# Later batches of x stored turned but unsplit, split when they come back, and setup's stores in another order

## What is computed

```python
proj = x @ W_in.T + b_in                      # W_in (3072, 256): q, k, v
q, k = _rope(q, sin, cos), _rope(k, sin, cos)
att = jnp.einsum('bhqd,bhkd->bhqk', q, k) * scale
att = jax.nn.softmax(jnp.where(mask, att, -inf), axis=-1)   # causal
y = jnp.einsum('bhqk,bhkd->bhqd', att, v)
...
return y @ W_out.T + b_out
x = _layernorm(x + attention(x))
x = _layernorm(x + experts(x))
```

## Time and profile before

| | us |
|---|---|
| median of 3 runs | 1839.72 |
| range of the runs | 1834.96 to 1841.53 |
| the profiled execution | 1837.63 |
| its span | 1834.3 |
| PE busy in the span | 1686.4 (92%) |
| DVE busy | 1383.9 (75%) |
| ACT busy | 722.0 (39%) |
| POOL busy | 1233.9 (67%) |

### The profile page before, as it was taken

The page is one execution under the profiler, slowest core; times in us unless marked ns, Lnnn a source line. Parts: engine busy times, 40 slices in busy tenths (PEclk is TensorE's granted clock), DMA queues, the critical chain, the costliest instruction groups (busy, mean ns, idle before and its releaser), DMA issues. The chain is left out here.

```text
span 1834.3 us, 34020 instructions
## 1 busy us (share of the span) xinstructions
PE 1686.4 (92%) x9515; PEld 1264.3 (69%) x9516; DVE 1383.9 (75%) x3235; ACT 722.0 (39%) x1519; POOL 1233.9 (67%) x1064
## 2 busy tenths in 40 slices
PE   4689999999999999999999999998659999999990
PEld 3556667666766677666766676664339999999980
DVE  3578888888888888988888898875776566656654
ACT  2234444444445544444444444543332222222222
POOL 3256788677877777788767787764017777777764
PEclk8799999999999999999999999999759999999995
DMA  9976556655665676456666565542974444444448
GB/s 307 336 207 162 154 168 199 182 164 157 184 163 156 209 205 179 140 160 187 199 188 187 166 188 142 161 127 98 355 241 72 71 73 74 71 73 74 71 65 278
DMA packets 185058, 302.36 MB, mean 165 GB/s; under 512 B 23120, under 2 KB 82384, under 8 KB 184800
## 3 DMA queue, kind: packets, MB, share of 16 engines
q1 hardware_dynamic: 161360, 269.20, 49.7%
q0 software_dynamic: 21504, 30.29, 10.4%
q10 hardware_dynamic: 2064, 1.31, 0.3%
HBM read 188.81 MB, written 111.67 MB: 164 GB/s over the span
## 5 line engine op out<-in xcount | busy, mean ns | idle before, releaser
L780 ACT ACTIVATE prob<-b_ps 128x512 f32<-128x512 f32 (+3 forms) x768 | 354.4, 488 | 360.3 <-PE b_ps L589 260.3
L516 POOL TENSOR_TENSOR acc<-acc,prob 128x1024 f32<-128x1024 f32 (+1 forms) x192 | 352.8, 1837 | 6.4 <-POOL acc L516 3.6
L588 PE MATMUL b_ps<-q,k 128*128 128x512 f32 (+3 forms) x768 | 296.1, 390 | 5.3 <-ACT prob L780 3.5
L489 POOL TENSOR_TENSOR roped<-rot 128x512 f32<-128x512 f32 x128 | 174.5, 1364 | 165.0 <-DVE rot L919 164.2
L581 PE MATMUL a_ps<-k,q 128*128 128x512 f32 (+3 forms) x768 | 265.8, 383 | 20.5 <-DMA k<-scratch_hilo 10.1
L670 PE MATMUL y_ps<-prob,v_sb 128*64 128x512 f32 (+3 forms) x1536 | 272.9, 490 | 0.1
L899 DVE CUSTOM_DVE_ANT_0 masked<-a_ps,causal 128x128 bf16<-128x128 f32 (+3 forms) x512 | 237.3, 479 | 45.9 <-PE a_ps L581 37.7
L589 PE MATMUL b_ps<-q,k 65*128 65x512 f32 (+3 forms) x768 | 264.4, 348 | 0.0
L1449 POOL DMA_INDIRECT scratch_sum<-y,dst_i x112 | 187.6, 1675 | 94.8 <-ACT y L1521 90.9
L948 DVE RECIPROCAL inv<-inv 128x128 f32<-128x128 f32 x256 | 232.2, 929 | 7.7 <-ACT inv L821 5.3
L494 POOL TENSOR_TENSOR lo<-roped,hi 128x512 fp32r<-128x512 f32 x128 | 176.8, 1382 | 80.6 <-ACT hi L793 80.6
(11 more groups left out here) (255 smaller groups left out, 2382.9 us busy)
## 6 DMA issues: line engine op xcount, KB each, us to landing
q<-scratch_hilo SPq DMA_DIRECT2D x192, 256.0 KB, 4.6
k<-scratch_hilo SPq DMA_DIRECT2D x192, 256.0 KB, 5.2
scratch_hilo<-hi SPq DMA_DIRECT2D x64, 512.0 KB, 3.8
scratch_hilo<-lo SPq DMA_DIRECT2D x64, 512.0 KB, 4.5
w_sb<-scratch_wsplit SPq DMA_DIRECT2D x32, 512.0 KB, 3.6
w<-in_L_ffn_W_dram SPq DMA_DIRECT2D x32, 512.0 KB, 9.9
wv_sb<-scratch_wsplit SPq DMA_DIRECT2D x16, 512.0 KB, 5.9
xT<-scratch_xsplit SPq DMA_DIRECT2D x6, 1024.0 KB, 6.2
```

Of the source, the lines that this page charges most:

```text
L516: nc.gpsimd.tensor_tensor(sums, old, probs(q), ALU.add).then_inc(m["sum_p"], 1)
L588: nc.tensor.matmul(out, k1[s][:, h, js], q1[s][:, h, qs], start=True, stop=False, skip_group_check=True)
L780: nc.scalar.activation(probs(q)[:, h, :], b_ps[:, h, 0:w], ACT.Exp).then_inc(exp_done[h], 1)
```

## The change

Batches 1, 2 and 3 of x are turned in setup and copied out of PSUM whole, in fp32, with no subtraction. They lie in `v_sb` (batch 1) and `prob` (2 and 3) and are stored in `xturned`, 1 MB each in one transfer. `load_x` brings a half of the tokens of such a batch (0.5 MB in place of 1 MB) into the low part of `xT`. There a new event, `s`, splits it: for each of the two k, ACT copies it to the high part, and DVE subtracts. `s0` and `s1` (the halves of the tokens) stand in the lists of ACT and DVE for the pair two turns ahead, and do something only where that pair is the first of a batch other than the first. F0 and F1 of such a pair wait for the split.

In setup, the six weight units that lie in buffers of pair 0 (`WAITED`: q and k of pairs 2 to 7) are stored first, with a semaphore of their own. The stacked loads of pair 0 wait only for these. The other six units (`OTHERS`) are stored in two groups of three, around the first stack. The halves of the second half of the tokens go out after them, and x last, in the order 2, 3, 1. PE no longer waits for the low parts of late units, and ACT no longer waits for the weight stores ahead of batch 3.

```diff
-ACT_ORDER = parse("""E0.0 E0.1 E1.0 E1.1 E2.0 w1 E2.1 E3.0 d1- h0++ N1- E3.1 E4.0 E4.1 y0 h1++ E5.0 d0 h2++ E5.1 E6.0 N0 E6.1 y1 E7.0
+ACT_ORDER = parse("""E0.0 E0.1 s0++ E1.0 E1.1 E2.0 w1 E2.1 E3.0 d1- s1++ h0++ N1- E3.1 E4.0 E4.1 y0 h1++ E5.0 d0 h2++ E5.1 E6.0 N0 E6.1 y1 E7.0
...
-DVE_ORDER = parse("""M11.1 M0.0+ C0 M0.1+ M1.0+ M1.1+ M2.0+ k0 M2.1+ M3.0+ k1 k2 r0++ M3.1+ R4- r1++ R5- M4.1+ k3 M4.0+ R6- R7-
+DVE_ORDER = parse("""M11.1 M0.0+ C0 M0.1+ s0++ M1.0+ M1.1+ M2.0+ k0 M2.1+ M3.0+ k1 k2 s1++ r0++ M3.1+ R4- r1++ R5- M4.1+ k3 M4.0+ R6- R7-
...
+        x_whole = [None] + [t.rearrange("p (k c) -> p k c", k=DK)
+                            for t in (v_flat[:, 0:DK * T], prob[:, 0:DK * T], prob[:, DK * T:2 * DK * T])]
...
+            def put_weights(units, stored):
+                for i in units:
...
+            put_weights(WAITED, wsp_first)
...
             def put_x(b):
                 sp.wait_ge(m["setup_hi"], NW + 4 * (b + 1))
-                sp.wait_ge(m["setup_lo"], NW + 4 * (b + 1))
-                dst = xsplit[b].rearrange("p (a k c) -> p a k c", a=2, k=DK)
-                for a in range(2):
-                    for k in range(DK):
-                        sp.dma_start(dst[:, a, k], x_place[b][a][k].bitcast(F32)).then_inc(xsp[b], 16)
+                sp.dma_start(xturned[b].rearrange("p (k c) -> p k c", k=DK), x_whole[b]).then_inc(xsp[b], 16)
...
             def load_x(batch, c):
-                sp.dma_start(xT[:, :, :, 512 * c:512 * c + 512].bitcast(F32),
-                             row(xsplit, batch).rearrange("p (a k c) -> p a k c", a=2, k=DK)
-                             [:, :, :, 512 * c:512 * c + 512]).then_inc(x_ld[c], 16)
+                sp.dma_start(xT[:, 1, :, 512 * c:512 * c + 512].bitcast(F32),
+                             row(xturned, batch).rearrange("p (k c) -> p k c", k=DK)
+                             [:, :, 512 * c:512 * c + 512]).then_inc(x_ld[c], 16)
...
-            for c in range(2):
-                put_halves(0, 0, c)
-            sp.wait_ge(m["wsp"], 16 * NW)
-            for c in range(2):
-                for second in range(2):
-                    stack(0, 0, c, second)
-                put_x(1 + c)
-            put_x(3)
+            put_halves(0, 0, 0)
+            put_weights(OTHERS[:3], m["wsp"])
+            sp.wait_ge(wsp_first, 16 * len(WAITED))
+            for second in range(2):
+                stack(0, 0, 0, second)
+            put_weights(OTHERS[3:], m["wsp"])
+            put_halves(0, 0, 1)
+            for second in range(2):
+                stack(0, 0, 1, second)
+            for b in (2, 3, 1):
+                put_x(b)
+            sp.wait_ge(m["wsp"], 16 * len(OTHERS))
...
-                    pe.wait_ge(m["setup_lo"], old + 1)
+                    if u < EARLY:
+                        pe.wait_ge(m["setup_lo"], old + 1)
...
-                        if q < 2 and not first:
-                            pe.wait_ge(x_ld[q], 16 * (n // PAIRS + 1))
+                        if q < 2 and n >= PAIRS:
+                            pe.wait_ge(m["setup_lo"], EARLY + splits_before(n, q) + 2)
...
+                    elif kind == "s":
+                        if n % PAIRS or n == 0:
+                            continue
+                        act.wait_ge(x_ld[q], 16 * (n // PAIRS + 1))
+                        for k in range(DK):
+                            nc.scalar.activation(xT[:, 0, k, 512 * q:512 * q + 512],
+                                                 xT[:, 1, k, 512 * q:512 * q + 512].bitcast(F32),
+                                                 ACT.Copy).then_inc(m["setup_hi"], 1)
...
+                    elif kind == "s":
+                        if n % PAIRS or n == 0:
+                            continue
+                        for k in range(DK):
+                            dve.wait_ge(m["setup_hi"], NW + NX + splits_before(n, q) + k + 1)
+                            low = xT[:, 1, k, 512 * q:512 * q + 512]
+                            nc.vector.tensor_tensor(low, low.bitcast(F32), xT[:, 0, k, 512 * q:512 * q + 512].bitcast(F32),
+                                                    ALU.subtract).then_inc(m["setup_lo"], 1)
...
-                        if n == 0 and q == 3:
-                            low_halves(EARLY, NW + NX)
```

More of the change, by code:

```diff
@@ L133, in attention_phase @@
     x, W_in, b_in, W_out, cosT, sinT = A["x"], A["W_in"], A["b_in"], A["W_out"], A["cos"], A["sin"]
-    xsplit, wsplit = dram["xsplit"], dram["wsplit"]
+    xturned, wsplit = dram["xturned"], dram["wsplit"]
     hilo = dram["hilo"]
@@ L189, in attention_phase @@
         m = {k: sem(k) for k in names}
-        xsp = [sem(f"xsp{b}") for b in range(B)]
+        wsp_first = sem("wsp_first")
+        xsp = [None] + [sem(f"xsp{b}") for b in range(1, B)]
         x_in = [sem(f"x_in{b}") for b in range(B)]
@@ L234, in attention_phase @@
                            next(later).rearrange("p (a k c) -> p a k c", a=2, k=DK))
[L235 to L241, removed]
+        v_flat = v_sb[:, 1].rearrange("p t s c -> p (t s c)")
+        x_whole = [None] + [t.rearrange("p (k c) -> p k c", k=DK)
+                            for t in (v_flat[:, 0:DK * T], prob[:, 0:DK * T], prob[:, DK * T:2 * DK * T])]
         def setup_places(u):
@@ L247, in setup_places, with splits_before @@
             b, k, c = X_UNITS[u - NW]
-            return [x_place[b][a][k][:, 512 * c:512 * c + 512] for a in range(2)]
+            cs = slice(512 * c, 512 * c + 512)
+            return [xT[:, a, k, cs] for a in range(2)] if b == 0 else [x_whole[b][:, k, cs]]
+        WAITED = [u for u in range(NW) if W_UNITS[u][0] == "qk" and 2 <= W_UNITS[u][1]]
+        OTHERS = [u for u in range(NW) if u not in WAITED]
+        def splits_before(n, c):
+            return 4 * (n // PAIRS - 1) + 2 * c
         late_banks = [b_ps[:, i, :] for i in range(2)] + [a_ps[:, i, :] for i in range(2)]
@@ L301, in _ @@
             sp.dma_start(wo_raw, W_out.rearrange("(r p) c -> p r c", p=P)).then_inc(m["wo_in"], 16)
[L303 to L307, removed]
+            def put_weights(units, stored):
+                for i in units:
+                    what, p = W_UNITS[i]
+                    sp.wait_ge(m["setup_hi"], i + 1)
+                    sp.wait_ge(m["setup_lo"], i + 1)
+                    sp.dma_start(wsplit[p if what == "qk" else PAIRS + p].rearrange("p (a k c) -> p a k c", a=2, k=DK),
+                                 w_place[i].bitcast(F32)).then_inc(stored, 16)
+            put_weights(WAITED, wsp_first)
             sp.wait_ge(m["setup_hi"], EARLY)
@@ L384, in turn @@
                     elif kind == "S":
-                        if n == 1 and c == 0:
-                            for b in range(1, B):
-                                sp.wait_ge(xsp[b], 64)
                         stack(n, s, c // 2, c % 2)
@@ L544, in late_transposes @@
                     transposes(NW + NX + i, [wo_raw[:, r, (4 * c + j) * P:(4 * c + j + 1) * P] for j in range(4)])
-                pe.wait_ge(m["setup_lo"], NW + NX)
                 pe.wait_ge(m["wo_ev"], len(WO_UNITS))
@@ L734, in high_halves @@
                     act.wait_ge(m["setup_tr"], u + 1)
-                    if u >= NW and X_UNITS[u - NW] == (3, 0, 0):
-                        act.wait_ge(m["wsp"], 16 * NW)
                     src = setup_bank(u)
@@ L762, in turn @@
                             for b in range(1, B):
-                                act.wait_ge(xsp[b], 64)
+                                act.wait_ge(xsp[b], 16)
                         act.wait_ge(b_fill[h], UNITS * n + q + 1)
@@ L1759, in scratch @@
 def scratch(nc):
-    shapes = {"xsplit": [B, P, 2 * DK * T], "wsplit": [PAIRS + PAIRS // 2, P, 2 * DK * 256], "hilo": [2, 2, P, 2, T], "xn": [NTOK, E_ + D]}
+    shapes = {"xturned": [B, P, DK * T], "wsplit": [PAIRS + PAIRS // 2, P, 2 * DK * 256], "hilo": [2, 2, P, 2, T], "xn": [NTOK, E_ + D]}
     shapes.update({f"sum{i}": [NTOK + P, D] for i in range(SUMS)})
```

## The result

| | before | after |
|---|---|---|
| median of four runs each, us | 1838.12 (1834.96 to 1841.53) | 1861.85 (1858.54 to 1864.55) |
| ratio after/before | | 1.0121, 95% interval 1.0104 to 1.0138 |
| profiled execution, its span, us | 1837.6, 1834.3 | 1864.55, 1860.8 |

The change costs 23.7 us. The forecast was 1850, its range ended at 1857. The direction was right, the size wasn't, and what follows is mainly about the twelve microseconds that the forecast lacked.

The account below looks back on a forecast made before the run. Queues bound the first 120 us, and PE, without slack, the turns. 1837.6 - 5.6 (start) - 0.3 (x loads) + 15.6 (splits) + 1.6 (clock) = 1848.9, by the median 1851.0; forecast 1850 us, 8-in-10 range 1838 to 1857.

Parts of the forecast that it names:

- the two holds: Boundary turns: PE held 2.1 us by the first split group, 3.1 by the second; +15.6 us over three boundaries.
- The turns of about 42 us: Predicted trace sign: turns of 36.7 us except three of about 42, those before batches 1, 2 and 3.
- rival (a): Boundary turns: the splits hide in DVE and ACT idle time, costing +2.0 to +3; 1834 us; chance 0.15.
- the term of the clock: Boundary turns: PE's granted clock falls after the 3.1 us hold; up to 1.6 a boundary, a third taken, +1.6 us.
- Rival (c): Boundary turns: the clock falls at both holds and stays low through a fill each; 1857 us; chance 0.08.
- the start: Setup and first turns: reordered stores, dropped subtractions and shorter queue waits gain 5.6 us, between -2 and -11.
- the x loads: Boundary turns: halving the load of x gives at most 0.2 us a boundary; -0.3 taken for the three.
- The wait of 4.24: Start, at 75.81 us: PE's wait for a stacked load; removal gives 0.3, late second stack gives back 0.7.
- The give-back: Start: the second stack lands at about 73 against a need at 71.8, returning up to 1.2 of 4.0 us.
- The two later waits on stacked loads: Start: PE's waits of 0.96 and 2.02 us behind the stores of split x go, counted 1.0 + 1.0, -2.0 us.
- rival d: Boundary turns: the second half-load of x isn't there in time, +1.3 us a boundary; 1853 us; chance 0.05.
- Rival (e): Start: engines serve queued stores and loads side by side, so the new order gains nothing; 1854 us; chance 0.05.

Follow-up runs that it names:

- the filled kernel: The changed kernel with matmuls that nobody reads put into PE's holds at the three batch boundaries; 1850.85 us, one run.
- The moved splits: The changed kernel with first-group split steps one turn earlier, second-group steps elsewhere in the ACT and DVE order, half-load of x ahead of wv's; 1838.73 us, ratio 0.9992 to before.
- the kernels with idle steps: Three kernels: the kernel before with 1, 2 or 3 unread DVE reductions ahead of M1.0 in three turns, lengths permuted; 1846.96, 1840.30, 1846.99 us.
- the order alone: The kernel before with only the new order of stores, x still split and stored in setup as before; 1847.22 us against 1840.11, ratio 1.0036.
- the first group alone: The changed kernel with only the first half of the tokens split at the boundaries, the second group's copies and subtractions left out; 1847.54 us, one run.

## Why the prediction missed

**Right: the two holds.** Forecast 2.1 and 3.1 us, measured 2.00 and 1.30 + 1.59; the releasers and their order were as described (the first held matmul was the one of 128x384, not 128x256). DVE's idle time before the third subtraction was forecast at 2.7 us and is 2.7 where no spell comes first; with the spell it was 3.2 to 4.2. The waits sum to 14.4, the filled kernel gives 15.9, forecast 15.6. The turns of about 42 us that the prediction named are the filled kernel's 42.13. Reading what stands *next* on each engine decided this; the 5 us of idle DVE per turn, rival (a), hid nothing at those places. The moved splits show that rival (a) is right at others.

**Wrong: the term of the clock.** I took +1.6 for the three boundaries, bounds 0 to 4.8. It measured 10.4 (the filled kernel) to 11.9 (the rest without a wait). Two errors are in it. The *count*: I gave a spell only to the longer hold, and there only in a third of cases, because one hold of 2.02 us in the trace of before kept its clock. That was a single case. At 1.8 to 2.0 us the clock falls most of the time (8 of 9), and in the changed kernel it did so behind both groups at all three boundaries. And the *size*: I took 1.6 us as the most for a boundary, from one fill at a mean clock of 0.62. A spell costs 1.4 us in the kernels with idle steps and 1.7 to 2.0 here, with two at each boundary, one of the six twice as long. Rival (c), with two spells of 1.6 us for each boundary (1857), is the case that happened, and it had 0.08. Its 1857 stands on the profiled execution's time; on the median's, as the forecast of 1850 nearly does, it is 1859, beyond the end of the range. From it to the profiled 1864.55 it is 2.3 more for the spells, 2.6 less gained at the start, 3.3 behind the turns, 0.3 for the x loads that gained nothing and 0.4 outside the span, less 1.2 for the holds. That each wait brought the lower clock is what the Trainium skill (TensorE: Matmul & The Clock Gate, HAM oscillation) tells of its own kernel, whose waits are some 3 to 5 us, so it isn't a rule for the shorter ones here. Of these, 17 of 18 holds by the splits had a spell behind them, and none of the six of 1.1 us and less.

**Right on average, less in this trace: the start.** Forecast -5.6, between -2 and -11; the profiled execution had -3.0, the mean of six traces has -6.3. First scores at 59.4 (59.94) and first max_c near 96 (96.8) were met. The wait of 4.24 stayed (4.20); the sum had its going at -0.3 and also +0.7 for its staying, which exclude each other. The give-back came from elsewhere than forecast: the row of maxima, 0 to 2.8 us by execution. The two later waits on stacked loads are gone. (The 2 us of fixed cost of one transfer, which the prediction took from the Trainium skill's page DMA: Bandwidth & Descriptors, stand there under Anatomy of one DMA, for transfers issued from GpSimd, and not under Bandwidth. No sum used them.)

**Right: the x loads** (rival d): half 1, issued at 316.86, landed at 324.97, 3.9 us before the copies took it. Rival (e) fell with the first scores at 59.94.

In sum, of the 12 us between 1850 and 1861.85 the clock is 9 to 10 (10.4 to 11.9, less the 1.6 that was in the forecast). The range was too narrow at the top: where a cost comes per event and its trigger isn't known, the bound is all the events, 6 x 1.6 = 9.6 us from the rows at hand, and I had used 4.8.

## What to carry to other kernels

Where TensorE has no slack, added steps on another engine are paid by their place, not by their number: look for what stands behind them on that engine and who waits for it. The same eight steps a boundary cost 26 us over the three boundaries at one place and some 4 at another. Count each hold of 1.7 us and more twice, once for itself and once for the slow work behind it, and look for the second in the granted clock, since PE is busy there and none of its waits shows it. And ask of two edits that come together whether one makes the other possible: the order of the stores was a gain only with whole x.

## What the runs showed of the hardware

- The granted clock after a hold varies between like cases: at the first group's place it fell behind 1.7 us twice in three, behind 1.8 to 2.0 us eight times in nine, behind 1.1 us and less never in six. What decides beside the length no run here shows.
- This bears on the spread of the kernel before too. The last turn but one waits for the row of maxima, 0.86 us in its trace, 1.65 with the order alone, and there the clock goes down as well. The stretches of before and of that kernel:

```profile
1221.00:1229.00 8.00, 7.83 (x40) 4.83 (x41) 4.52 (x11) 3.85 (x7) 2.37 (x1) 1.00 0.00 1
```

```profile
1221.80:1228.60 6.80, 5.94 (x17) 2.75 (x19) 4.05 (x8) 1.66 (x3) 0.00 (x0) 0.57 0.00 0
```

  That turn is 33.0 to 33.5 us in seven of the thirteen traces and 34.6 to 36.5 in six, and just the six have a spell in it. Their waits for the row are 0.74 to 1.76 us, those of the seven 0.76 to 1.32, each followed some 3 us later by one of 0.9 to 1.3 for a maximum of DVE's. So 0.74 and 1.26 us close together brought a fall once (with the first group alone), where 1.32 and 1.25 did not:

```profile
1223.85 0.47 PE L595 MATMUL b_ps<-q,k 128*128 128x512 f32 x1 [0.74 <-DMA q<-mrow]
...
1226.73 0.33 PE L588 MATMUL a_ps<-k,q 128*128 128x128 f32 x1 [1.26 <-DVE max_b L918]
```

```profile
1227.70:1231.10 3.40, 3.40 (x12) 1.20 (x11) 1.41 (x4) 0.60 (x1) 0.00 (x0) 0.50 0.00 0
```

  The limit of 1.1 us above was found for a single hold in a full turn and doesn't hold here. That this turn makes part of the 1833.8 to 1847.1 us over which runs of the kernel before spread is likely, but wasn't tested.
- PE waited for a DMA of 4 KB until some 7 us after its issue while another queue loaded in bulk; the same row of maxima is waited for between 0 and 2.8 us at the start, by execution (six traces with the changed setup).
